# First and last expert turns split into two passes of two tiles, and the down product with t as stationary block

## What is computed

```python
x = x + wkv(w, u, layernorm(x), ctx)      # per channel, over the positions:
#   y = (A*p + E*v) / (A*q + E);  p, q, o = decayed sums of E2*v, E2 and the running maximum
h = layernorm(x)                           # 1024 tokens of 256
probs = softmax(h @ gate_w)                # 32 experts
w, sel = top_k(probs, 8); w = w / sum(w)   # a token is dropped where the expert is full
g = einsum('ech,ehi->eci', h_of_slot, w_gate);  u = the same with w_up     # 96 inner columns
y = einsum('eci,eih->ech', silu(g) * u, w_down)
x = x + sum over the chosen experts of w * y
```

## Time and profile before

| | |
|---|---|
| runs, median of 3 | 268.7 us (268.12 to 270.14) |
| the profiled execution, time | 269.1 us |
| its span | 266.8 us |
| PE busy, PEld busy | 243.9 us (91%), 186.9 us (70%) |
| DVE, ACT, POOL busy | 134.8, 134.3, 161.1 us |
| granted clock, mean | 0.976 |

### The profile page before, as it was taken

The page is one execution under the profiler, slowest core; times in us unless marked ns, Lnnn a source line. Parts: engine busy times, 40 slices in busy tenths (PEclk is TensorE's granted clock), DMA queues, the critical chain, the costliest instruction groups (busy, mean ns, idle before and its releaser), DMA issues.

```text
span 266.8 us, 3968 instructions
## 1 busy us (share of the span) xinstructions
PE 243.9 (91%) x1058; PEld 186.9 (70%) x1061; DVE 134.8 (51%) x342; ACT 134.3 (50%) x242; POOL 161.1 (60%) x140
## 2 busy tenths in 40 slices
PE   6636798799999999999999999999999999999993
PEld 1412486677678777778687778787878787878772
DVE  4598887339562794439643534235342332424333
ACT  2766453576366753594377635343525353435320
POOL 5118202856768565858586675858677686868610
PEclk9999879799999999999999999999999999999998
DMA  7950500006050524124050505050505060700002
GB/s 208 258 147 22 156 26 0 0 0 185 16 154 22 135 64 121 56 50 127 10 169 6 173 1 161 17 153 26 156 21 166 13 173 17 222 22 0 1 0 79
DMA packets 43359, 22.23 MB, mean 83 GB/s; under 512 B 34128, under 2 KB 43344, under 8 KB 43344
## 3 DMA queue, kind: packets, MB, share of 16 engines
q1 hardware_dynamic: 42496, 21.63, 28.1%
q10 hardware_dynamic: 848, 0.43, 0.6%
HBM read 21.01 MB, written 1.05 MB: 83 GB/s over the span
## 4 chain that ended last, share of the span: by engine, by line
PE 68%; DVE 14%; ACT 6%; issue 6%; POOL 4%; DMA 1%; DVEq 0%; POOLq 0%; ACTq 0%
PE bank L699 40%; PE bank L717 8%; PE bank L721 7%; PE bank L718 7%; DVE t_sb L1042 3%; DVE bank L911 2%; DVE inv L922 2%; POOL rstd L357 2%; DVE t_sb L1048 2%; PE bank L616 2%; PE bank L657 2%; PE bank L706 1%; ACT normed L446 1%; DMA x_sb<-in_x_dram 1%; POOL t_lo L375 1%
## 5 line engine op out<-in xcount | busy, mean ns | idle before, releaser
L375 POOL TENSOR_TENSOR t_lo<-t_sb,t_hi 128x512 fp32r<-128x512 f32 x47 | 60.8, 1294 | 75.1 <-ACT t_hi L542 75.1
L349 POOL TENSOR_TENSOR wlo<-raw,whi 128x768 fp32r<-128x768 f32 x48 | 88.5, 1847 | 6.7 <-ACT whi L505 6.5
L699 PE MATMUL bank<-h_hi,whi 128*128 128x512 f32 x192 | 80.8, 421 | 0.3 <-issue 0.3
L1042 DVE TENSOR_TENSOR t_sb<-bank,s_sb 128x512 f32<-128x512 f32 x48 | 33.1, 690 | 93.4 <-PE bank L706 45.8
L699 PE MATMUL bank<-h_lo,whi 128*128 128x512 f32 x192 | 76.7, 400 | 0.0
L699 PE MATMUL bank<-h_hi,wlo 128*128 128x512 f32 x192 | 76.2, 397 | 0.0
L542 ACT ACTIVATE t_hi<-t_sb 128x512 fp32r<-128x512 f32 x48 | 30.3, 630 | 90.9 <-DVE t_sb L1048 90.9
L505 ACT ACTIVATE whi<-raw 128x768 fp32r<-128x768 f32 x48 | 40.0, 835 | 8.6 <-PE bank L721 8.6
L699 PEld LDWEIGHTS bank<-h_hi,whi 128*128 128x128 f32 x192 | 36.9, 192 | 8.8 <-issue 0.8
L699 PEld LDWEIGHTS bank<-h_hi,wlo 128*128 128x128 f32 x192 | 36.6, 191 | 8.8
L699 PEld LDWEIGHTS bank<-h_lo,whi 128*128 128x128 f32 x192 | 36.8, 192 | 8.0
(11 more groups left out here) (120 smaller groups left out, 194.0 us busy)
## 6 DMA issues: line engine op xcount, KB each, us to landing
raw<-in_L_ffn_w_gate_dram SPq DMA_DIRECT2D x16, 384.0 KB
raw<-in_L_ffn_w_up_dram SPq DMA_DIRECT2D x16, 384.0 KB
raw<-in_L_ffn_w_down_dram SPq DMA_DIRECT2D x48, 128.0 KB
out_dram<-x SPq DMA_DIRECT2D x4, 256.0 KB, 2.5
x_sb<-in_x_dram SPq DMA_DIRECT2D x1, 512.0 KB, 7.0
ctx_tile<-in_ctx_dram SPq DMA_DIRECT2D x4, 128.0 KB, 5.2
x_sb<-in_x_dram SPq DMA_DIRECT2D x1, 256.0 KB, 3.4
ctx_sb<-in_ctx_dram SPq DMA_DIRECT2D x1, 256.0 KB, 4.6
```

The lines of the kernel that those rows point to most:

```text
L349: pool.tensor_tensor(split_view(wlo, slot, part), raw_parts(slot, part), split_view(whi, slot, part).bitcast(F32), ALU.subtract).then_inc( ...
L375: pool.tensor_tensor(t_lo[k % 2][:], t_sb[:], t_hi[k % 2][:].bitcast(F32), ALU.subtract).then_inc(t_lo_ready, 1)
L699: last = nc.tensor.matmul(ps[:], up_weight(w, slot, part, k, j), h[:, k, tokens], start=(i == 0), stop=(i == len(terms) - 1))
L1042: nc.vector.tensor_tensor(t1_sb[:], w_ps[:], s_sb[:], ALU.mult).then_inc(t1_ready, 1)
```

## The change

- The turns 0 of both halves and the last turn of the second half run twice over the same two groups, in passes of two tiles (256 columns): pass 0 takes tiles 0 and 1 of the half, pass 1 tiles 2 and 3. The other five turns stay whole. A pass has 6 half-steps; the weights are split once for both passes.
- The first step needs the first unit only. The second unit is routed beside pass 0 of turn 0, on PE at half-steps 1, 3 and 5; its route is needed at pass 1. The second unit is added to x and gets its statistics on DVE ahead of step 0.
- `early` is gone: the four one-tile units are mixed beside turns 0 (pass 1) to 3 of the first half and each routed a turn later, the last one beside pass 0 of the second half's first turn. None of them inverts by Ln and Exp now.
- In the prologue ACT and DVE are reordered; ACT and POOL also split the second group's weights there.
- `down` takes a 128x128 block of t as stationary operand and the 256 columns of w_down's block as moving ones: 12 products a whole step, 6 a half-step, each into its tile's y. y comes out with tokens as rows; the copy, the transposes and the tile `y_sb` go, and `add_output` reads y from PSUM.
- The first two output tiles of a half are added while the rest is computed.
- SP issues the next context tile after the reloads of a turn instead of ahead of them. PE's loops over turns are written out. PSUM banks are assigned anew.

The diff, cut to its core:

```diff
+        first_units = [Unit(n, NT * n, NT, n, (n, n + 2), False, by_log=True) for n in range(2)]
...
+        LATER = range(2, 2 + HT)
...
-        early = Unit(2, HT, 1, 2, (2, 5), True, by_log=True)
...
+        PASSES = (0, 1)
+        WHOLE = (None,)
+        HALF_STEPS = GROUPS * GT + TURN_STEPS
+        ALL_STEPS = 2 * HALF_STEPS + TURN_STEPS
...
+        def steps_of_last_user(half, it, ahead):
+            again = 1 if not half or (isinstance(it, int) and it == 0 and ahead == 1) else 2
+            return it * TURN_STEPS + ((half * GROUPS + ahead - 1) * GT + again * TURN_STEPS)
...
+        def down_weight(w, slot, j):
+            return w[slot][:, 2, j * C:(j + 1) * C]
...
             for half in range(2):
                 with sp.Fori(0, TURNS - 1) as it:
+                    for slot in range(2):
+                        reload(half, slot, it, it * 2 + (2 + slot))
                     if half == 0:
                         load_context(it + 3)
-                    for slot in range(2):
-                        reload(half, slot, it, it * 2 + (2 + slot))
...
                 pool.wait_ge(w_hi_ready, group * 3 + part + 1)
-                if not isinstance(group, int) or group >= 2:
-                    pool.wait_ge(down_done, (group - 1) * GT + 2)
+                if users_done is not None:
+                    pool.wait_ge(down_done, users_done + 2)
                 pool.tensor_tensor(split_view(wlo, slot, part), raw_parts(slot, part),
...
+            def turn(half, it, passes, beside={}, split=(1, 2), leave_last=False):
+                for p in passes:
+                    for k in range(TURN_STEPS):
+                        if not (leave_last and p == 1 and k == TURN_STEPS - 1):
+                            product_low(steps_before(half, it) + (p or 0) * TURN_STEPS + k, k, p)
+                        for stage in beside.get((p or 0, k), []):
+                            stage()
+                        ahead = k // GT + 1
+                        if ahead in split and p in (None, ahead - 1):
+                            split_low(ahead % 2, k % GT, it * 2 + (half * GROUPS + ahead), steps_of_last_user(half, it, ahead))
...
+            turn(0, 0, PASSES, {(0, 0): [lambda: power(third, third.first_norm)]}, split=(2,))
...
+            turn(1, TURNS - 1, PASSES, split=(1,), leave_last=True)
...
             decay_factors(NT, factors[0])
             bonus_gain()
-            exps(first_units[0])
-            norm_x(first_units[1])
-            exps(first_units[1])
-            norm_x(early)
-            decay_factors(1, factors[1])
+            exps(first)
+            norm_x(second)
+            exps(second)
+            invert(first)
             act.wait_ge(gate_landed, 16)
             nc.scalar.activation(gate_hi[:], gate_sb[:], ACT.Copy).then_inc(gate_hi_ready, 1)
-            invert(first_units[0])
-            exps(early)
             for part in range(2):
                 split_high(0, part, 0)
-            invert(first_units[1])
+            spread_experts()
             split_high(0, 2, 0)
-            spread_experts()
-            for u in first_units:
...
+                                    (0, 2): [lambda: take_h(back)],
+                                    (0, 3): [lambda: exps(front), lambda: route_exps(routed), lambda: fetch_silu(it * 2)]})
...
+            turn(0, 0, PASSES, {(0, 0): [lambda: take_route(first_routed), lambda: norm_h(second)],
+                                (0, 1): [lambda: norm_x(third)],
+                                (0, 2): [lambda: take_h(second)],
+                                (0, 4): [lambda: exps(third), lambda: route_exps(second_routed), lambda: fetch_silu(0)],
+                                (1, 0): [lambda: take_route(second_routed)]}, split=(2,))
+            later_turn(1)
+            with act.Fori(2, TURNS) as it:
+                later_turn(it, later_routed(it))
+            turn(1, 0, PASSES, {(0, 0): [lambda: take_route(later_routed(LATER[-2]))],
+                                (0, 1): [lambda: norm_h(last)],
...
+                turn(1, it, WHOLE)
+            turn(1, TURNS - 1, PASSES, split=(1,))
...
+            def down(n, p, slot, j, odd, group, last_of=None):
...
+                tiles = range(HT) if p is None else range(p * NT, (p + 1) * NT)
+                def product(t, a, b, stop=False):
+                    at = (t - tiles[0]) * P
+                    return nc.tensor.matmul(y_tile(t), a[odd][:, at:at + P], down_weight(b, slot, j), start=False, stop=stop)
+                for t in tiles:
+                    product(t, t_hi, whi)
+                    product(t, t_hi, wlo)
...
+                for t in tiles:
+                    last = product(t, t_lo, whi, last_of is not None and t % NT == NT - 1)
+                    if last_of == 0 and t == NT - 1:
+                        last.then_inc(y_ready, 1)
                 last.then_inc(down_done, 1)
...
+                        elif k < TURN_STEPS - 1:
+                            project(n + 1, half, p, 0, (k + 1) // GT, (k + 1) % GT, group + (k + 1) // GT)
+                        elif p == 0:
+                            if half and first_turn:
...
+                            project(n + 1, half, then_pass, 0, 0, 0, group + 2)
+                        for stage in beside.get((p or 0, k), []):
+                            stage()
+                        if first_turn and k == 0:
+                            if half:
+                                pe.wait_ge(out_ready, p + 1)
+                            start_sum(p)
+                        if k > 0:
+                            down(n - 1, p, (k - 1) // GT, (k - 1) % GT, (k - 1) % 2, group + (k - 1) // GT)
+                        elif p == 1:
+                            down(n - 1, 0, 1, GT - 1, 1, None, last_of=1 if last_turn else None)
+                        elif not first_turn:
+                            down(n - 1, 1 if it == 1 else None, 1, GT - 1, 1, None)
+                        for stage in after.get((p or 0, k), []):
...
+            turn_mixed(first)
             keep_clock(12)
...
+            turn_h(first)
+            logits(first_routed)
+            project(0, 0, 0, 0, 0, 0, 0)
+            project(0, 0, 0, 1, 0, 0, 0)
+            project(1, 0, 0, 0, 0, 1, 0)
+            turn_mixed(second)
+            turn_parts(first_routed)
+            third, last, last_routed = later(2), later(LATER[-1]), later_routed(LATER[-1])
+            turn(0, 0, PASSES, {(0, 1): [lambda: turn_h(second)],
+                                (0, 2): [lambda: turn_kv(third)],
+                                (0, 3): [lambda: logits(second_routed)],
+                                (0, 5): [first_counts],
+                                (1, 5): [lambda: turn_mixed(third)]},
...
+            for it in range(1, TURNS):
+                later_turn(it)
+            down(HALF_STEPS - 1, None, 1, GT - 1, 1, None, last_of=0)
+            turn(1, 0, PASSES, {(0, 1): [lambda: turn_h(last)], (0, 2): [lambda: logits(last_routed)]},
...
+                turn(1, it, WHOLE, then_pass=0 if it == TURNS - 2 else None)
+            turn(1, TURNS - 1, PASSES)
+            down(ALL_STEPS - 1, 1, 1, GT - 1, 1, None, last_of=1)
...
-            recur(first_units[0])
-            stats_x(early)
-            recur(first_units[1])
-            for u in first_units:
-                mix(u)
...
+            fractions(first, *sums_done)
+            weighed = begin_sums(second)
+            refine(first)
+            mix(first)
+            q_done = scan_keys(second)
+            add_mixed(first)
+            p_done = scan_values(second, weighed)
+            fractions(second, q_done, p_done)
             dve.wait_ge(gate_hi_ready, 1)
...
+            h_low(first)
+            refine(second)
+            largest(first_routed)
+            mix(second)
+            choose(first_routed)
+            weigh(first_routed)
+            add_mixed(second)
...
+            def add_output(half, q):
...
+                    rows = x1[:, half * HT + t, :]
+                    last = nc.vector.tensor_tensor(rows, rows, y_tile(t), ALU.add)
+                last.then_inc(out_ready, 1)
...
+            turn(0, 0, PASSES, {(0, 0): [(stats_x, third)],
+                                (0, 2): [(h_low, second)],
+                                (0, 3): [(largest, second_routed)],
+                                (0, 4): [(choose, second_routed)],
+                                (0, 5): [(weigh, second_routed), (count_first, None)],
+                                (1, 0): [(all_sums, third)],
+                                (1, 2): [(all_fractions, third)],
+                                (1, 3): [(end_sums, third)],
+                                (1, 4): [(mix, third)]})
...
+            dve.wait_ge(y_ready, 1)
+            add_output(0, 0)
+            add_mixed(last)
+            dve.wait_ge(down_done, HALF_STEPS + 2)
```

(9 more changed lines are left out.)

471 lines of the change are left out of this document (191 added, 280 removed).

## The result

| | before | after |
|---|---|---|
| median of the runs | 268.6 us (268.12 to 270.14) | 275.7 us (275.03 to 276.37) |
| ratio | | 1.024 (1.0203 to 1.0278) |
| span of the profiled execution | 266.8 us | 274.6 us |
| PE busy, PEld busy | 243.9, 186.9 us | 248.9, 215.7 us |
| granted clock, mean | 0.976 | 0.948 |

The account below looks back on a forecast made before the run. After the prologue PE's work was taken as the bound; -7.7 + 1.6 + 3.2 + 2.4 + 0.8 + 2.1 + 3.9 - 1.4 = +4.9 us gave 273.6 us. Likeliest range 268 to 278, whole range 263.5 to 283.

Parts of the forecast that it names:

- the third cost: About 47 to 53 us in the kernel before: PE at seven tenths and a granted clock of 0.7.
- Pace of PE: Split turns: 256-column pairs 0.118 us apart, against 0.2328 for 512 columns; +1.6 us.
- Rival B: Split turns: pairs at the load's floor of 0.111, stalls as forecast; 266.6 us, chance 0.10.
- C: Split turns: a fixed 0.02 paid for each load, 0.127 a pair; 282.7 us, chance 0.17.
- D: Split turns: load and stream share what they read, 0.140 a pair; 295.8 us, chance 0.09.
- The start: Prologue: first t1 at 35.0 against 42.99, first down product about 38.0 against 49.24; -7.7 us net of halves owed.
- Work under PE and half-steps, first turn: Work moved from the prologue to where PE is the bound, +3.2 us; first-turn stalls, cold clock and norms, +2.4.
- Third whole turn: It now has a unit in front too: a stall of about +0.8 us.
- Change of half: Between halves: PE waits about 1.0 for t and 2.0 for the norm, transposes go (-0.9); +2.1 us net.
- Seams: Split turns: PE waits 1.3 us for POOL's low weights at three places, hidden behind the norm at a fourth; +3.9.
- The end: Tail: no copy or transposes, last chain on halves; 4.3 us against 5.4, and less waiting (-0.3); -1.4.
- Rival A: PE's order has slack enough, so 10.1 us of half-step stalls vanish; 263.5 us, chance 0.17.

Follow-up runs that it names:

- x1: Changed kernel with the last unit added on DVE ahead of the wait for y and the output adds at the change of half: 273.32 us, 1.0125.
- x2: Changed kernel with eight bf16 products of zeros on PE ahead of the last unit's transposes, filling its wait for the norm: 273.55 us, 1.0131.
- x6: Changed kernel with the last unit added ahead of the wait for y and the last turn whole: 272.22 us, 1.0112.
- x7: Changed kernel without the last unit's mixing, norm and routing (its h and route zeros, so that output is wrong): 270.14 us, 1.0057.
- x8: As x6, with the last unit's way from its transposes of h on one half-step later: 273.11 us, 1.0153.
- x3: Changed kernel with the last turn whole, as in the kernel before, instead of in two passes: 273.07 us, 1.0137.
- x5: Kernel before with h zero, so project and down products have zeros as moving operand (output wrong): 269.66 us, 1.0000.
- x9b: Kernel before with the new down product and output, and ACT's prologue reordered as in the change: 267.21 us, 0.9927.

## Why the prediction was nearly right, point by point

- **What bounds the kernel.** Right. The whole turns of the second half are PE busy without a gap (49.44 of 49.44). Only the reading "from the eighth slice on" is off: the eighth slice of the earlier trace rows has seven tenths, the one that I named as the third cost, and the nines begin with the ninth.
- **Pace of PE.** Right, 0.118. The step that decided was the logits' 0.111 with no surplus, read as "the surplus goes with the stream". The forecast's 0.118 had no working of its own between 0.116 and 0.127, so that it is met to the last digit is luck. Rival B (0.111), C (0.127) and D (0.140) are all wrong. The Trainium skill (TensorE: Matmul & The Clock Gate, Back-to-back issue gap) has a pair at 128 columns cost more than the isolated matmul; the estimate of 0.134 that I had worked out from it for 256 columns is not borne out here, since 0.118 was measured.
- **The start.** Right: first t1 35.4 for 35.0, first down product 38.2 for 38.0.
- **Work under PE and half-steps, first turn.** Too dear by 3.3 over the stage. I had 1.2 for a cold clock after PE's idle time; the clock was low from 34.2 to 37.6 only, ahead of the first down product, whose time of 38.2 already holds it, so I had counted it twice. I had 3.1 for ACT's block in the fifth half-step; its two waits are 0.2 and 1.55 (the row below has 1.39 of it). And I had 1.3 for the seam; it shows 0.34. These come to 3.5 (1.2, 1.3 and 1.0), and the late 0.2 of the first down product goes the other way. The cold clock is this execution's: in x1, x2 and x6, the same code up to here, the clock was low until 42.6, 41.5 and 42.5, and the spread of turn 1 came at 70.65, 69.69 and 70.70. The forecast has 71.5 for this spread (72.78 less 1.3), only 0.8 to 1.8 more than these three, so a part of the 3.3 belongs to this execution's clock.

PE of the kernel after in order of time, around the fifth half-step:

```profile
51.78 0.31 PE L693 MATMUL bank<-ident_bf,parts 128*96 128x128 bf16 x2 [1.39 <-DVE parts L1037]
```

- **Third whole turn.** About right: the waits of turns 1 to 3 are 3.3 together, against 2.1 before, so +1.2 for +0.8.
- **Change of half, its waits.** Right in mechanism and size: t ends at 158.58, 3.3 behind the end of the half's last down product at 155.32 (forecast 3.3), gaps of 0.84 and 1.69 (1.0 and 2.0).
- **Change of half, the clock.** This is the step that failed. In the first turn I had charged idle time with a slow clock behind it; at the change of half, where my own steps open two gaps close together, I charged nothing for it, and the clock fell: 3.7 us by x2, in this execution. Of the 4.9 by which the turn is over its terms, the clock is 3.7. Another 0.7 is PE's wait for the last unit's choosing (line 1017), which I had not priced either.
- **Seams.** The mechanism is right (PE waits for POOL's wlo, 1.27 at the worst), the size too large: 0.34, 0.34 and 0.30, 0.34 and 1.27 come to 2.6 for 3.9. "Hides behind the wait for the norm" was right, and x7 and x8 show what it costs without that cover: 1.7 and 2.2.
- **The end.** Better than forecast: from the last down product (its end at 271.3) to the end of the span it is 3.3, where I had 4.3 (before: 5.4). But x3, with the last turn whole, is 1.8 faster over the last two turns and the tail, so the split loses at its seams (0.34 and 1.27) more than its shorter last chain and the earlier adds bring. In my sum the two nearly balanced (-1.4 and +1.3).
- **Rival A** (stalls hidden) is wrong: it needed the stalls under 2.6 together, and the second half's first turn alone has 5.0 of waits.

**Where the gain went.** The start is 7.6 earlier, net of the halves owed, and this gain is real. Of it, 5.3 is left at the end of the first turn (4.6 by the spreads, and 0.7 less is owed there). The second half's first turn then takes 9.7 more (11.85 less the 2.1 of the cut): 3.7 the clock, 5.0 waits (0.94, 1.85, 0.24, 0.24, 0.89, 0.19, 0.34 and 0.30, each a start that comes late against the pace), 1.3 the routing of the last unit, which the old kernel had done a turn earlier, 0.35 pace, and -0.9 for the `turn_output` that went: 9.5. The root is that a unit of mixing fell on the first half-steps of a split turn, where PE has 2.1 us of work between the points at which it needs something, and the chain for one unit takes longer than that.

What stays open: why the granted clock was low for 10.24 us in one execution and for 3.41 in another of the same code at the same place, and whether it always falls there (that it held in x1, x2, x6, x7 and x8 is one trace each, and x7 and x8 have two gaps there too, of 0.55 and 0.83 and of 1.43 and 0.58, their ends 2.5 apart); and whether a version with whole turns and the first unit ahead on PE would keep the 7.6.

## What to carry to other kernels

Price a split of a pipeline step not by its products, which cost 1.6 us here, but by what stands beside one step and doesn't halve: a norm, a weight split, a router. When a change opens two idle gaps of PE a few us apart, reckon a fallen clock as a case of its own (here it fell in two of four kernels with such gaps); a few products of zeros in the gap show at once what it costs. And try the parts alone: the plain part here (t as stationary block, no transposes at the end) is worth 0.5% to 1.1% by itself, and the rest of the change lost about 3%.

## What the runs showed of the hardware

- fp32r products of 128x128 by 512 columns stand 0.233 apart at the granted 2.4 GHz and those of 256 columns 0.118, with a change of weights before each; with 32 columns it is 0.111. bf16 with 512 columns takes 0.216. Zeros as the moving operand change nothing (x5).
- At the 1.2 GHz level 256 columns take 0.213 (after, behind 162.02), 512 columns 0.43, and 32 columns 0.213 as well (the logits of x9b, 32.66 and 32.88). By these rows 32 columns behind a load of 128x128 cost 0.111 and 0.213, and 256 columns cost hardly more, so it looks as if the load set the floor at both levels; no run changed the load.
- The granted clock fell with gaps of 0.84 and 1.69 whose ends lay 2.7 us apart, in the second gap (after) or 0.8 behind it (x3). It held with one of 1.69 (x1, x6), with the second one filled (x2), and with pairs of 0.55 and 0.83 (x7) and 1.43 and 0.58 (x8). For the same code the fall lasted 10.24 us once and 3.41 once. The Trainium skill (TensorE: Matmul & The Clock Gate, What's actually happening) says, of the start of a kernel, that the same kernel shows different numbers of slow products from run to run. The prologues of these two kernels, which are the same code, agree with it: the clock was low from 10.33 to 20.57 in the kernel after and from 12.85 to 19.68 in x3.
